# Attention with mixture-of-experts: half of O^T stored whole in fp32 and split in the output stage, and the output bias as one product of 128 rows

## The reference

```python
xn = _layernorm(x)
Q, K, V = xn @ Wq + bq, xn @ Wk + bk, xn @ Wv + bv      # per head; Q, K hold two halves of 64
P = softmax(Q1 K1^T * s) - lam * softmax(Q2 K2^T * s)
O = P @ V                                               # per head, 512 x 64
Y = concat(O) @ Wo + bo                                 # 4096 x 1024 times 1024 x 256
attn = ((Y - mean(Y)) * rsqrt(var(Y) + 1e-5) * gamma + beta) * 0.2
route = argmax(softmax(xn @ switch_w + switch_b)); prob = its maximum
ffn = (gelu(xn @ w1[route] + b1[route]) @ w2[route] + b2[route]) * prob
out = x + attn + ffn
```

## Time and profile before

| | |
|---|---|
| median of 3 runs | 1900.21 us (1899.0 to 1900.91) |
| profiled execution, its own time | 1900.06 us |
| its span, first to last instruction | 1898.0 us |
| busy share of the span: PE, DVE, ACT, POOL | 97%, 81%, 74%, 38% |
| attention, about | up to 1485 us |
| feed-forward, about | 1485 to 1771 us |
| output stage, about | 1771 to 1898 us |

### The profile page before, as it was taken

How to read it: one execution, slowest core, us unless ns; L and a number is a source line. 1 busy time by engine, 2 the same in 40 slices (tenths; PEclk the granted TensorE clock), 3 DMA queues, 4 the chain that set the end, 5 groups by cost and what they waited for, 6 DMA issues and landing times. The chain is left out here.

```text
span 1898.0 us, 33183 instructions
## 1 busy us (share of the span) xinstructions
PE 1832.6 (97%) x10688; PEld 1423.4 (75%) x10688; DVE 1536.0 (81%) x2562; ACT 1397.8 (74%) x3287; POOL 719.6 (38%) x805
## 2 busy tenths in 40 slices
PE   5899999999999999999999999999999799999997
PEld 4677777777777777777777777777767599999886
DVE  7798888888888888888888888889977476666365
ACT  6798888888888888888888888888777476666100
POOL 4344223232223323323332223332392475554343
PEclk9999999999999999999999999999999799999999
DMA  9998888888888888888888888888876476676998
GB/s 310 252 254 244 237 226 230 226 224 227 233 225 227 229 214 226 225 231 226 228 230 224 226 228 227 229 230 224 211 200 181 138 285 238 235 234 215 310 369 274
DMA packets 226164, 446.11 MB, mean 235 GB/s; under 512 B 27937, under 2 KB 116897, under 8 KB 220001
## 3 DMA queue, kind: packets, MB, share of 16 engines
q1 hardware_dynamic: 220992, 429.86, 81.0%
q0 software_dynamic: 5024, 14.42, 2.5%
HBM read 184.40 MB, written 58.46 MB: 128 GB/s over the span
## 5 line engine op out<-in xcount | busy, mean ns | idle before, releaser
L604 ACT ACTIVATE e<-p_score,nmax 128x512 f32<-128x512 f32 x1024 | 697.2, 689 | 138.6 <-DVE nmax L836 138.2
L455 POOL TENSOR_SCALAR e<-e,rrec,lam 128x512 f32<-128x512 f32 x512 | 393.7, 769 | 948.6 <-DVE rrec L796 948.6
L836 DVE TENSOR_REDUCE nmax<-p_score 128x2 f32<-128x1024 f32 x512 | 623.3, 1217 | 152.7 <-PE p_score L945 150.9
L945 PE MATMUL p_score<-ks,qs 128*128 128x512 f32 x2048 | 578.8, 404 | 8.3 <-DMA ks<-k_parts 5.1
L945 PEld LDWEIGHTS p_score<-ks,qs 128*128 128x128 f32 x2048 | 365.3, 188 | 178.5 <-issue 52.0
L803 DVE SCALAR_TENSOR_TENSOR pm<-e,rrec 128x512 f32<-128x512 f32 x512 | 395.3, 772 | 10.5 <-issue 9.9
L908 PE MATMUL p_proj<-xh,w 128*128 128x512 f32 x1024 | 387.1, 419 | 7.5 <-POOL xl L433 4.6
L537 ACT COPY pT<-p_tr 128x512 f32<-128x512 f32 x512 | 301.0, 588 | 113.8 <-PE p_tr L957 113.8
L957 PE MATMUL p_tr<-consts,pm 128*128 128x128 f32 x2048 | 310.0, 274 | 3.2 <-ACT pT L537 2.3
L957 PEld LDWEIGHTS p_tr<-consts,pm 128*128 128x128 f32 x2048 | 250.2, 141 | 80.2 <-issue 20.0
L972 PE MATMUL p_pv<-pT,v 128*64 128x512 f32 x1024 | 249.2, 608 | 0.7 <-ACT pT L537 0.7
(11 more groups left out here) (158 smaller groups left out, 1876.5 us busy)
## 6 DMA issues: line engine op xcount, KB each, us to landing
ks<-k_parts SPq DMA_DIRECT2D x512, 256.0 KB, 4.6
qs<-q_parts SPq DMA_DIRECT2D x512, 128.0 KB, 4.4
w<-weight_parts_scratch SPq DMA_DIRECT2D x56, 1024.0 KB, 10.6
w<-in_w SPq DMA_DIRECT2D x46, 1024.0 KB, 6.7
oT_scratch<-oT SPq DMA_DIRECT2D x64, 512.0 KB, 6.2
op<-oT_scratch SPq DMA_DIRECT2D x32, 1024.0 KB, 10.2
wv<-weight_parts_scratch SPq DMA_DIRECT2D x56, 256.0 KB, 5.6
weight_parts_scratch<-w SPq DMA_DIRECT2D x8, 1024.0 KB, 6.3
```

Source lines behind the costliest of these rows:

```text
L455: nc.gpsimd.tensor_scalar(e2, e2, rrec[:, g % 4, 1:2], lam[:, 0:1], ALU.mult, ALU.mult).then_inc(s_e2, 1)
L604: nc.scalar.activation(ex[:, g % EX, m, :], p_score[g % 2][:, m, :], ACT.Exp, bias=nmax[:, g % 2, m:m + 1], accum_out=rsum[:, g % 4, m:m + ...
L836: vec.tensor_reduce(nmax[:, g % 2, :], p_score[g % 2][:, :, :], AXX, ALU.max, negate=True).then_inc(s_max, 1)
L945: last_op = nc.tensor.matmul(p_score[g % 2][:, m, :], qs[j][u][:, m, qt * P:(qt + 1) * P], ks[j][u][:, m, part, :], start=(part == 0), sto ...
```

## The change

Pairs 0 to 3 of each batch ("whole") are stored as fp32, 256 KB instead of 512 KB; VectorE makes no low part of them in the attention stage. Pairs 4 to 7 ("parts") are stored as before. In the output stage SP loads for a group one DMA of 512 KB of whole pairs into one of two buffers `of`, and two DMAs of 512 KB of parts into `op`. ScalarE makes the high part of the whole pairs (`high_o`, 128 x 1024), VectorE the low part (`low_o`, 128 x 1024). The bias's high part sits in row 0 and its low part in row 32 of `bop`, all else zero, so one product with 128 contraction rows of ones takes the place of two with one row; to build it, ScalarE rounds the rows, VectorE writes the two rows to `bo_rows`, and ScalarE copies them to `bop`.

```diff
             def store_o(pair):
...
+                if whole(pair):
+                    sp.dma_start(oW_d[h, :, a:b], oT_whole[:, :]).then_inc(s_ost, 16)
+                else:
+                    sp.dma_start(oP_d[h - WHOLE, :, :, a:b], oT[:, :, :].bitcast(F32)).then_inc(s_ost, 16)
...
-                nc.scalar.copy(oT[:, 0, :], p_pv[:, :]).then_inc(s_ohi, 1)
+                if whole(pair):
+                    nc.scalar.copy(oT_whole[:, :], p_pv[:, :]).then_inc(s_o, 1)
+                else:
+                    nc.scalar.copy(oT[:, 0, :], p_pv[:, :]).then_inc(s_ohi, 1)
...
-                if st == 2 and pair >= 2:
+                if st == 2 and pair >= 2 and not whole(pair - 2):
                     low_o(pair - 2)
...
+        def op_free(engine, n):
+            if n == 0:
+                engine.wait_ge(s_h, HG * (FFN_TILES - 1))
+            elif n == 1:
+                engine.wait_ge(s_w2lo, FFN_TILES)
+            elif n == 2:
+                engine.wait_ge(s_y, FFN_TILES - 1)
+            else:
+                engine.wait_ge(s_oy, n - OPS + 1)
...
-            def load_o(n):
+            def load_whole(n):
+                if n >= 2:
+                    sp.wait_ge(s_ohi, n - 1)
+                    sp.wait_ge(s_olo, n - 1)
+                sp.dma_start(of[n % 2][:, :, :], oW_v[:, :, n * G:(n + 1) * G]).then_inc(s_of[n % 2], 16)
+            def load_parts(n):
+                op_free(sp, n)
                 for c in range(2):
-                    sp.dma_start(op[n % OPS][:, c, :, :].bitcast(F32), oT_v[:, c, :, n * G:(n + 1) * G]
+                    sp.dma_start(op[n % OPS][:, c, WHOLE:PAIRS, :].bitcast(F32), oP_v[:, c, :, n * G:(n + 1) * G]
                                  ).then_inc(s_op[n % OPS], 16)
...
             turns(body, before_last=first_o)(sp)
-            sp.wait_ge(s_w2lo, FFN_TILES)
-            load_o(2)
+            load_parts(2)
+            load_parts(1)
+            load_whole(2)
             store(FFN_TILES - 1, 0)
...
-                    sp.wait_ge(s_oy, n + 1)
-                    load_o(n + OPS)
+                    load_whole(n + OPS)
+                    load_parts(n + OPS)
...
-                nc.scalar.copy(bop[:, 0, :], rows[0:1, 0, :]).then_inc(s_wohi, 1)
+                nc.scalar.copy(bop[:, :], rows[:, 0, :]).then_inc(s_wohi, 1)
                 act.wait_ge(s_ones, 1)
                 nc.scalar.copy(ones_r[:, :], ones[:, :]).then_inc(s_wohi, 1)
+                act.wait_ge(s_bo, 2)
+                nc.scalar.copy(bop[:, :], bo_rows[:, :]).then_inc(s_wohi, 1)
+            def high_o(n):
+                act.wait_ge(s_of[n % 2], 16 * (n // 2 + 1))
+                op_free(act, n)
+                nc.scalar.copy(op[n % OPS][:, 0, 0:WHOLE, :], of[n % 2][:, :, :]).then_inc(s_ohi, 1)
             turns(body, after_third=output_weights)(act)
+            for n in range(OPS):
+                high_o(n)
             nc.scalar.activation(warm[:, :], consts[:, 0:4], ACT.Sqrt)
             for q in range(GROUPS // 2):
+                for n in (2 * q + OPS, 2 * q + OPS + 1):
+                    if n < GROUPS:
+                        high_o(n)
...
+                v.tensor_copy(bo_rows[0:1, :], bop[0:1, :].bitcast(F32)).then_inc(s_bo, 1)
+                v.tensor_tensor(bo_rows[BO_LOW:BO_LOW + 1, :], rows[BO_LOW:BO_LOW + 1, 0, :],
+                                bop[BO_LOW:BO_LOW + 1, :].bitcast(F32), ALU.subtract).then_inc(s_bo, 1)
...
+            def low_o(n):
+                dve.wait_ge(s_ohi, n + 1)
+                v.tensor_tensor(op[n % OPS][:, 1, 0:WHOLE, :], of[n % 2][:, :, :],
+                                op[n % OPS][:, 0, 0:WHOLE, :].bitcast(F32), ALU.subtract).then_inc(s_olo, 1)
             turns(body, after_third=output_weights)(dve)
+            for n in range(OPS):
+                low_o(n)
             add_b2(FFN_TILES - 1, 0, LOOPED // 2, False)
...
                     if done[0] == RECIPROCAL_STEP:
+                        if 2 * q + OPS < GROUPS:
+                            low_o(2 * q + OPS)
                         base(2 * q)
...
                     normed(2 * q + c)
+                if 2 * q + OPS + 1 < GROUPS:
+                    low_o(2 * q + OPS + 1)
...
                 pe.wait_ge(s_op[c], 32 * (n // OPS + 1))
+                pe.wait_ge(s_olo, n + 1)
...
-                    for part in range(2):
-                        nc.tensor.matmul(p_o[r][:, s, :], ones_r[:, :], bop[:, part, :],
-                                         start=(part == 0), stop=False)
+                    nc.tensor.matmul(p_o[r][:, s, :], ones_r[:, :], bop[:, :], start=True, stop=False)
```

More of the change, by code:

```diff
@@ L96, with front_stage @@
 FIRST_SHIFT = MOMENT_STEPS + 1
-def front_stage(nc, ins, wp_d, xn_d, oT_d, consts, slot_u, prob, tile_expert, token, ahead, s_ost):
+def front_stage(nc, ins, wp_d, xn_d, oW_d, oP_d, consts, slot_u, prob, tile_expert, token, ahead, s_ost):
     with ExitStack() as ctx:
@@ L155, in front_stage @@
         pT = [pTs[0:2], pTs[2:4]]
+        with ExitStack() as early:
+            oT_whole = early.enter_context(nc.sbuf_tensor("oT_whole", [P, S], F32))
         counts = [2 * (b - a) for a, b in TURNS]
@@ L220, in batch_of, with whole, parted @@
             return pair // PAIRS
+        def whole(pair):
+            return pair % PAIRS < WHOLE
+        def parted(pair):
+            return pair // PAIRS * (PAIRS - WHOLE) + pair % PAIRS - WHOLE + 1
         def weights(j, part, what, u, k):
@@ L1062, in gather, with ffn_and_output_stage @@
             ).then_inc(self.landed["xs"][n % 2], 16)
-def ffn_and_output_stage(nc, ins, ys_d, oT_d, consts, tile_expert, slot_u, prob, ahead, s_oT, out):
+def ffn_and_output_stage(nc, ins, ys_d, oW_d, oP_d, consts, tile_expert, slot_u, prob, ahead, s_oT, out):
     with ExitStack() as ctx:
@@ L1092, in ffn_and_output_stage @@
         sb("w1p_home", [P, 2, KT, F])
-        op1, op0, op2 = (sb(f"op{c}", o_shape, F32R) for c in (1, 0, 2))
+        op0 = sb("op0", o_shape, F32R)
+        of = [sb(f"of{c}", [P, WHOLE, G]) for c in range(2)]
+        sb("of_home", [P, 2 * (KT * F - WHOLE * G)])
+        op1 = sb("op1", o_shape, F32R)
         sb("loads_home", ahead.rest)
-        op = [op0, op1, op2]
         w2p = [sb(f"w2p_{j}", [P, 2, FT, E], F32R) for j in range(2)]
@@ L1098, in ffn_and_output_stage @@
         (h,), acc = then([("h", [P, HG, 2, FFN_TILE], F32)], [(f"acc{r}", [P, 2, E], F32) for r in range(R)])
-        hp = [sb(f"hp{j}", [P, 2, FT, FFN_TILE], F32R) for j in range(2)]
+        hp0 = sb("hp0", [P, 2, FT, FFN_TILE], F32R)
+        (hp1,), (op2,) = then([("hp1", [P, 2, FT, FFN_TILE], F32R)], [("op2", o_shape, F32R)])
+        hp, op = [hp0, hp1], [op0, op1, op2]
         y = [sb(f"y{j}", [P, FS, E]) for j in range(2)]
         wo, wop = sb("wo", [P, PAIRS, E]), sb("wop", [P, 2, PAIRS, E], F32R)
-        rows, bop = sb("rows", [P, 3, E]), sb("bop", [1, 2, E], F32R)
-        ones, ones_r = sb("out_ones", [1, P]), sb("ones_r", [1, P], F32R)
+        BO_LOW = 32
+        rows, bo_rows, bop = sb("rows", [P, 3, E]), sb("bo_rows", [P, E]), sb("bop", [P, E], F32R)
+        ones, ones_r = sb("out_ones", [P, P]), sb("ones_r", [P, P], F32R)
         gamma, beta = rows[:, 1, :], rows[:, 2, :]
@@ L1122, in ffn_and_output_stage @@
         s_wohi, s_wolo, s_bo = sem("o_wohi"), sem("o_wolo"), sem("o_bo")
-        s_op = [sem(f"o_op{c}") for c in range(OPS)]
+        s_op, s_of = [sem(f"o_op{c}") for c in range(OPS)], [sem(f"o_of{c}") for c in range(2)]
+        s_ohi, s_olo = sem("o_hi"), sem("o_lo")
         s_x, s_ff, s_ost = ([sem(f"o_{w}{r}") for r in range(R)] for w in ("x", "ff", "st"))
```

40 lines of the change are left out of this document (21 added, 19 removed).

## The result

The changed kernel takes 1893.3 us (median of 7 runs, 1890.71 to 1896.73) against 1900.91 us (7 runs, 1899.0 to 1903.19): ratio 0.9959, 95% interval 0.9948 to 0.9971, 7.6 us faster. The forecast was 1891.3, its range 1885 to 1898. The profiled execution took 1893.18 us, its span 1891.0 against 1898.0.

What follows compares the result with a forecast made beforehand. TensorE was taken to bound attention and the output stage, with the DMAs a little near its end. 1898.0 + 0 + 3.2 - 15.4 + 1.9 + 1.5 = 1889.2 us span, with 2.06 around it 1891.3; range 1885 to 1898.

Steps and rivals of the forecast that it cites:

- Attention: Attention stage: VectorE's 21.8 us less work is covered by TensorE's matmul queue; 0 us, bounds 0 and -5.4.
- The bias's preparation: Feed-forward tile 3: ScalarE waits for VectorE's two rows, TensorE stops 2.15 us, the clock may fall; +3.2 us.
- The bias product: Output stage on TensorE: one 128-row product replaces two one-row ones, saving 0.30 us a half; 9.7 us over 32 halves.
- The loads: Output stage: loads per group shrink, DMA time 6.34 us instead of 7.75, so 5.2 us of waits for op go.
- DMA would be below its full share: Output stage: a sign expected in the profile after the change, beside no waits for op.
- The loop: Output stage, once per quarter: root, normed, low_o, load, landing, high_o, root; 7.1 + L, TensorE 1.9 us late.
- the late start: Output stage's start: three low_o precede the last add_b2; store and gathers 3.5 us later, VectorE's first base some 1.5.
- waits of more than 5 us: Output stage: TensorE's waits at even groups for low_o, root behind a landing; summing above 5 us, they refute the prediction.
- VectorE itself: Output stage: two low_o bring VectorE's work per quarter to 10.7 us of TensorE's 12.6.
- The mild loop: Rival, output stage: with L between 7 and 8.8 us the loop only eats the gain; 1893 to 1904 us; chance 0.13.
- VectorE as the bound: Rival, output stage: GpSimd's additions stretch quarters up to 13.3 us; 1894 to 1896; chance 0.12 together with dearer bias product.
- The rule on VectorE and GpSimd excluding one another: Two-port or two-SBUF-input VectorE and SBUF-reading GpSimd instructions exclude one another; low_o can be held in the output stage.

Runs made afterwards that it cites:

- e4: Changed kernel with ScalarE's square root of quarter q put ahead of high_o(2q+4), on chip A: 1884.56 us, ratio 0.9922.
- e9: Changed kernel with the square root ahead of high_o(2q+4), run again on chip C: 1889.36 us, ratio 0.9933.
- e12: Changed kernel unaltered, run again on chip C: 1895.39 us, ratio 0.9965.
- e5: Changed kernel unaltered, run again on chip B: 1894.63 us, ratio 0.9962.
- e3: Changed kernel with ScalarE's last copy to bop and its wait moved behind the last feed-forward tile, on chip A: 1894.99 us, ratio 0.9971.
- e6: Changed kernel with all of the bias's preparation moved behind the last feed-forward tile, on chip B: 1899.02 us, ratio 0.9985.
- e1: Kernel before with only the bias part of the change, on chip A: 1901.91 us, ratio 1.0009.
- e2: Changed kernel with the bias as before (two one-row products), on chip A: 1892.46 us, ratio 0.9966.
- e7: Changed kernel with all bias preparation behind the last feed-forward tile and the square root ahead of high_o(2q+4), on chip B: 1895.67 us, ratio 0.9967.

## Why the prediction was right, point by point

**Attention, 0.** Right. VectorE's freed time, 17.0 us and not 21.8, was hidden, and TensorE busy 1364.00 instead of 1364.56 us.

**The bias's preparation, +3.2.** Right in place, mechanism and size: 2.15 us of stop were foreseen and 2.08 came, and tile 3 to tile 4 is 3.39 us longer. The clock fell as assumed, but it need not: in e4 the 24 products behind the same stop took 3.10 us, and the tile 1.5 us less. In the other five traces with this stop it fell. I took the price from one wait, and that wait's own price changed: the last 48 products of p_y took 7.45 us before and 6.02 after, behind the same wait of 2.46. That gave 1.5 us that the prediction has no term for.

**The bias product, -9.7.** The mechanism was right, the size too small: 0.51 us a half and not 0.30, 16.2 us in place of 9.7. I priced what the one-row products took themselves and held the 24 others at 0.126 us; those fell to 2.82 / 24 = 0.118. The Trainium skill (TensorEngine Tiling (Array Packing), "Key Properties") says that a change of tiling mode drains the engine; the runs are in line with this and add that a good part of the price stands in the neighbours' rows.

**The loads, 5.2 us of waits gone.** Right. That DMA would be below its full share was wrong for the middle of the stage (1.06, 357 GB/s from 1850 to 1860):

```profile
1850.00:1860.00 10.00, 8.85 (x74) 8.50 (x73) 9.79 (x23) 1.05 (x1) 4.92 (x5) 1.00 1.06 357
```

TensorE's faster halves ask for more per us, and used what the smaller loads gave back; the estimate of 6.34 us of DMA time a group is above TensorE's real 5.9, and in e4 the DMAs are full for 50 us.

**The loop, +1.9, and the late start, +1.5.** The loop was found with its parts, and its period was right: 13.8 us predicted (L = 6.7), 13.6 measured with landings of 6.4. But against TensorE's quarter of 11.8 us (2 x 5.9), not 12.6, the same loop loses more. In the stage it costs 3.8 us of waits and 1.4 us of slow clock behind one of them, 5.2 in place of 3.4. These are idle times up to modelled ends; by the distances between the starts of halves the same five places cost 6.3 us, and the pair e9 and e12 gives 6.0. The prediction named waits of more than 5 us as the sign that it is wrong: here they are 3.8 us, in e5 4.4, but in e12, the same kernel, 6.6, so by its own sign one trace of three speaks against its size of the loop. They stand at odd groups too, where the prediction looked at even ones. Most of what the cheaper bias product frees is lost here, as long as the loop stands. The late start was under-sized too: add_b2 came 5.9 us later, not 3.5, since the load that the third `low_o` hangs on took up to 8.5 us behind four loads of parts where the prediction put 6.7; what of the 5.2 is due to it, no run tells apart.

**VectorE itself, 10.7 of 12.6.** Too small: 12.3 us a quarter in e4, where it is no longer hidden behind the loop. Part of it are the holds beside GpSimd's additions: in the changed kernel's trace `base` takes 0.66 us each in the mean and `result` 0.63, against 0.56 and 0.51 before, 56 of them in seven quarters.

**Not foreseen: the halting, +5.7, and the tail, +2.4.** With halves of 2.94 and the loop the stage would have been 94.1 + 5.2 = 99.3; the halting brings it to 105.0, and 2.0 us that lie in the starts behind the waits and in slightly longer halves to 107.0. VectorE, not TensorE, sets the pace at the end, so the tail behind TensorE's last product is 13.11 instead of 10.74 us. The sum, 1889.2 predicted and 1891.0 measured, comes out near because errors cancel: -6.6 (the halves), -1.5 (the clock before the stage), -2.2 (chance up to tile 3 and after), +0.2 (tile 3), +1.8 (the loop), +5.7, +2.4 and +2.0, together +1.8. Direction and the mechanisms that the prediction named were right; the closeness of the size was luck in good part: the halting alone, which has no term in it, is 5.7 us beside 8.9 us of forecast gain.

**The rivals.** The mild loop, "it only eats the gain", describes what happened, at a lower L than it named, because TensorE was faster. Its bounds don't follow from the prediction's own terms, though: by 17.45 + 5 (7.1 + L) + 3.5 an L of 8.8 gives 1901.8 us and not 1904, and the kernel is slower than before from L = 8.5 on. VectorE as the bound was in reach only once the loop was cut (e4), and there the full DMAs stand beside it. The rule on VectorE and GpSimd excluding one another (the Trainium skill, SBUF — State Buffer, "Who interferes with whom") was weighed for `low_o`, which was not held in the output stage (1.22 to 1.27 us; one of the two ahead of the stage, at the same time as instructions of GpSimd, lasted 2.84). The traces agree with the rule elsewhere: `base` and `result` beside GpSimd's additions in the output stage, and 5.03 and 5.57 us in the feed-forward stage of e3 and e6.

## What to carry to other kernels

Two savings on two resources that take turns at the bound are to be priced together: alone the cheap product gave nothing (e1) and the small loads 7 us (e2; 5.3 of them in the output stage), and together they were held by a third thing, an in-order queue where a small, urgent operation (the root) stood behind a copy that waits for a DMA. Look for such loops through an in-order engine and put the urgent operation first: swapping them gave 6 us in the one pair whose runs don't overlap, against 7.6 for the change itself. And when a wait is removed, look up what it was keeping back: without the stop in tile 3, GpSimd's subtraction landed on VectorE's critical steps and cost more than the stop.

## What the runs showed of the hardware

- Products of 128 rows between one-row products take 0.126 us each, without them 0.118; the whole half 3.45 against 2.94.
- TensorE halted in one place of the output stage, 2.4 to 8.0 us, in every trace from two chips and in none from a third, with no releaser in the trace. It begins at full DMA load (a share of 1.07) while gathers land, and ends in eight of nine traces within half a us of their last packet; no packet of the instruction queues moves meanwhile. The cause stays open.
- After a stop of 2.06 to 2.08 us the granted clock fell to 0.50 in five traces and not in the sixth; and one wait of 2.4 to 2.5 us, before the last p_y, was followed by 48 products in 6.01 to 6.02 us in ten traces and 7.45 to 7.52 in four (before, e3, e6, e7). In the output stage one wait of 1.81 us has the clock below 1.00 behind it (0.59 from 1838 to 1842, the changed kernel), one of 1.86 us has not (1.00 from 1874 to 1876, e6). What decides, no run shows: the second stop went alike in all traces of one kernel, the first did not (e4 and e9). A price taken from one such stop is uncertain by its whole size, about 1.5 us.
- A VectorE subtraction of 0.68 us lasted 5.03, and one of 1.21 us 5.57, when GpSimd's subtraction ran at the same time.
